# Cross-attention and a ternary feed-forward: the context and Wkv turned by transposes, with work moved between slots and engines

## The chip, the cores and the metric

The kernel runs on one core of one Trainium2 chip. The metric is device microseconds of one execution. The five engines are named as in the profile: PE (TensorE matmul), PEld (TensorE weight load, beside PE), DVE (VectorE), ACT (ScalarE), POOL (GpSimd) and SP (SyncE, which here only starts DMAs).

## What is computed

The input is x, 16 x 56 tokens of 256 channels, and a context whose first 56 rows per batch are used, with 64 channels. The layer is cross-attention and then a feed-forward network whose weights are rounded to -1, 0 and 1 and whose activations are rounded to 8 bits:

```python
kv = latent_kv @ Wkv_expand.T                 # K and V, 256 columns each
k, v = jnp.split(kv, 2, axis=-1)
scores = jnp.einsum('bhqd,bhkd->bhqk', qh, kh) * inv_sqrt_d   # 16 heads of 16, causal
attn = jax.nn.softmax(scores, axis=-1)
x = x + attention(layernorm(x), ctx) @ Wout.T
x = x + qlinear(silu(qlinear(y, w_gate)) * qlinear(y, w_up), w_down)   # y = layernorm(x)
# qlinear: weights round(w / mean|w|) in -1..1, activations round(x * 127 / max|x|)
```

## The kernel before

**Tiles.** The 896 tokens are 7 tiles of 128. Attention goes by 8 pairs of batches (index `u`). The work is cut into slots 0 to 17 and a slot -1 for the start. In slot s below 8 the PE makes `scores(s)`, the transposes of the shifted scores of pair s-1 (`tr`), the products with V (`pv`), the transposes of the attention of pair s-2 (`aT`), the output projection of one token tile (`op`), and the jobs that the table `MISC_JOBS` lists for that slot. From slot 8 on (`GU0`) tile s-8 goes through gate and up products, tile s-10 through the transposes of the rounded gated values (`ht`), and tile s-11 through the down product (`dn`).

**Orders by hand.** Each engine has its own program in a fixed order. The PE writes all small products into four PSUM banks in turn: job number n goes to bank n mod 4 and waits (`take_bank`) until the job four before it has been read. ACT reads a job's bank unless `VECTOR_READS` lists it, in which case DVE does. Both read in the order of the jobs (`read_misc`). A reader of an SBUF tile waits for the bank read that filled it (`wait_read`).

**The start.** Wkv lies in `wkv_sb` with row 4p+o on partition p; the context lies in `ctx_sb` with two key positions of 64 channels side by side. `wkvT` holds Wkv turned, channels on partitions, once on partitions 0 to 63 and once on 64 to 127; `ctxT` holds the context turned, batches 0 to 7 on the lower half of the partitions and 8 to 15 on the upper half. In the kernel before, both are made by matrix products with the identity as moving operand, with an output on either half of the partitions: two jobs `wkvT` (one for K, one for V; 8 products each) and two jobs `ctxT` (4 products each). Each has one read of 128 partitions. An fp32 product stands as two instructions in the trace, a transpose as one.

**Masked K.** The scores need K with other heads set to zero (`k_wide`). For context half 0 the readers of the K products write it from the bank (`WIDE`); for half 1 the product is copied to `kT` and POOL widens it later (`WIDENINGS`).

**Weights.** The three feed-forward weights are loaded by SP (`f0`, `f1`, `f2`), their absolute sums are taken by ACT or DVE (`ABS_SLOTS`), the PE makes the means (`MEAN_SLOTS`), POOL scales and rounds them (`ROUND_SLOTS`), ACT takes the signs (`SIGN_SLOTS`), and three DMA transposes bring them into `wT` and `wdT`. SP's list has one entry `hold`, a wait for Wkv's arrival ahead of the second x load.

**Feed-forward.** Per tile ACT makes silu of the gate product (L677), DVE multiplies by the up product (L885) and takes the maximum (L892), then the tile is rounded in two halves by the engines that `ROUNDER` names (L336), transposed, and multiplied down. `FINISHER` says whether DVE adds scale and residual in one instruction (L925), or ACT scales (L699) and POOL adds (L584).

Of the kernel before, what the change touches and what calls it, by code (L numbers as in the profile page):

```python
# [5 lines left out]
ALU = mybir.AluOpType  # L6
# [53 lines left out]
VECTOR_READS = [('k', 0, (0, 1), (0, 1)), ('xT', 4), ('v', 2), ('q', 1, 2), ('k', 0, (1, 4), (0,)), ('xT', 2), ('xT', 3), ('ctxT', 0),  # L60
 ('k', 1, (0, 4), (0,)), ('woT', 0)]
# [10 lines left out]
SUB_BEHIND = {0: 2, 1: 3, 2: 12, 3: 4}  # L72
# [8 lines left out]
WIDENINGS = {0: [(1, 0, 0)], 1: [], 2: [(1, 1, 0), (1, 1, 1)], 3: [], 4: [(1, 0, 1)], 5: []}  # L81
# [5 lines left out]
ROUNDER = [('gpsimd', 'gpsimd'), ('gpsimd', 'gpsimd'), ('gpsimd', 'gpsimd'), ('gpsimd', 'gpsimd'),  # L87
           ('gpsimd', 'gpsimd'), ('gpsimd', 'gpsimd'), ('vector', 'scalar')]
# [5 lines left out]
FINISHER = ['gpsimd', 'gpsimd', 'gpsimd', 'vector', 'vector', 'vector', 'vector']  # L94
# [6 lines left out]
def xattn_ffn(nc, x, ctx_512, wq, wkv, wout, w_gate, w_up, w_down, out):  # L101
# [72 lines left out]
    with ExitStack() as ctx:  # L174
# [92 lines left out]
        misc_written = sem("misc_written")  # L267

# [72 lines left out]
        def load(eng, name):  # L341
            kind, i = (name[:-1], int(name[-1])) if name[-1].isdigit() else (name, 0)
            if kind == "hold":
                eng.wait_ge(wkv_in, 16)
                return
            if kind == "x":
                a, b = X_PARTS[i]
                eng.dma_start(x_sb[:, a:b, :], x_v[:, a:b, :]).then_inc(x_in[i], 16)
            elif kind == "ctx":
                eng.dma_start(ctx_sb[S // 2 * i:S // 2 * i + S // 2, :, :],  # L350
                              ctx_512[i::4, 0:S, :].rearrange("b (k e) l -> k b (e l)", e=2)).then_inc(ctx_in, 16)
            elif kind == "wkv":
                eng.dma_start(wkv_sb[:, :, :], wkv.rearrange("(p o) c -> p o c", o=4)).then_inc(wkv_in, 16)
            elif kind == "wq":
                eng.dma_start(wq_sb[:, :, :], wq.rearrange("(o p) c -> p o c", p=P)).then_inc(wq_in, 16)
            elif kind == "wo":
# [5 lines left out]

        def read_misc(eng, copy, job):
# [4 lines left out]
            if kind == "wkvT":  # L368
                last = copy(wkvT[:, C * i:C * i + C], bank[:, 0:C])
            elif kind == "ctxT":  # L370
                last = copy(ctxT[:, KT // 2 * i:KT // 2 * i + KT // 2].rearrange("l (k e) -> l e k", e=2),
                            bank[:, 0:KT // 2].rearrange("l (e k) -> l e k", e=2))
# [6 lines left out]
            elif kind == "k" and job in WIDE:  # L379
# [3 lines left out]
                for hf in job[3]:  # L383
                    last = nc.vector.tensor_tensor(k_wide[:, i, hf, :, 2 * S * j0:2 * S * j1],
                                                   bank[:, None, width * (hf - hfs[0]):width * (hf - hfs[0]) + width].to_broadcast([P, RH, width]),
                                                   head_mask[:, 0:RH, None].to_broadcast([P, RH, width]), ALU.mult)
# [579 lines left out]
        def _(pe):  # L966
# [9 lines left out]
            def write_values(i):  # L976
# [3 lines left out]
                wait_read(pe, ("wkvT", 0), ("wkvT", 1), ("ctxT", 0), ("ctxT", 1))  # L980
# [13 lines left out]
            def write_misc(job):  # L994
# [6 lines left out]
                if kind == "wkvT":  # L1001
                    const(pe, "ident")
                    pe.wait_ge(wkv_in, 16)
                    for o in range(4):
                        for c in range(2):
                            last = mm(bank[Q * c:Q * c + Q, o:C:4], wkv_sb[:, o, :], ident[:, Q * i:Q * i + Q],
                                      start=True, stop=True)
                elif kind == "ctxT":
                    pe.wait_ge(ctx_in, 64)
                    for e in range(2):  # L1010
                        for c in range(2):
                            last = mm(bank[Q * c:Q * c + Q, 2 * S * e:2 * S * e + 2 * S],
                                      ctx_sb[:, 2 * c + i, L * e:L * e + L], ident[0:2 * S, 0:2 * S], start=True, stop=True)
                elif kind == "k":
# [3 lines left out]
                    wait_read(pe, ("wkvT", 0), ("ctxT", 0), *[("ctxT", 1)] * (j1 > 2))  # L1018
# [235 lines left out]
```

## Time and profile before

| | us |
|---|---|
| median of 3 runs (88.12 to 88.43) | 88.37 |
| the profiled execution, time | 88.7 |
| its span, first to last instruction | 86.9 |
| PE busy | 79.3 (91%) |
| DVE busy | 69.1 (80%) |
| ACT busy | 53.8 (62%) |
| POOL busy | 48.5 (56%) |

The page gives, for the chain that ended last, PE 57%, DVE 17%, POOL 8%, time without a wait 7%, DMA 4%, ACT 3%. A busy share is a mean over stretches that differ: the page's 40 slices show PE at nine tenths or more nearly to the end, and DVE at nine tenths in the last third. So the rows further down are read by stretch, not from the totals. The profiled execution is 0.33 us above the median; what is worked out from its rows is a difference to it, and is carried over to the median.

### The profile page before, as it was taken

Reading aid. Unit: us, or ns where it says so; the run is one execution under the profiler, and the core shown is the slowest. Engines: PE = TensorE matmul, PEld = TensorE weight load, DVE = VectorE, ACT = ScalarE, POOL = GpSimd, SP = SyncE. Lnnn points to the kernel's source line nnn. Section 1 sums busy time; section 2 is a strip of 40 time slices with the busy share of each in tenths; the row PEclk is TensorE's granted clock in tenths of the full one; section 3 lists DMA queues with packets and bytes.
Section 4 is the critical chain, followed back from the end, with each engine's and each line's share of the span. In section 5 each row is a group of like instructions: output and inputs, shape, how many; then the busy total and the mean of one; then the engine's idle time right before and its main releaser. Section 6 shows DMA issues by size and latency. Waiting matters only on the chain.

```text
span 86.9 us, 2805 instructions
## 1 busy us (share of the span) xinstructions
PE 79.3 (91%) x1068; PEld 57.9 (67%) x1068; DVE 69.1 (80%) x161; ACT 53.8 (62%) x96; POOL 48.5 (56%) x119
## 2 busy tenths in 40 slices
PE   4999999999999999999999899999996989998850
PEld 1387646679888797879888787675642656765630
DVE  4712799699699947999689986659999999999850
ACT  0625321699179737785219997973459969885620
POOL 5640378790891002989469877500989847669000
PEclk9999999999999999999999999999999999999999
DMA  0779999910000000006500092800000000101152
GB/s 26 217 234 316 322 379 370 352 70 8 0 4 8 0 11 0 0 8 130 116 0 8 0 241 55 194 0 0 0 0 0 8 0 0 60 0 60 64 173 69
DMA packets 11748, 7.60 MB, mean 88 GB/s; under 512 B 6552, under 2 KB 11480, under 8 KB 11736
## 3 DMA queue, kind: packets, MB, share of 16 engines
q1 hardware_dynamic: 11068, 6.93, 26.5%
q10 hardware_dynamic: 668, 0.51, 1.9%
q8 instruction: 8, 0.13, 0.6%
q14 instruction: 4, 0.03, 0.1%
HBM read 4.95 MB, written 0.92 MB: 68 GB/s over the span
## 4 chain that ended last, share of the span: by engine, by line
PE 57%; DVE 17%; POOL 8%; issue 7%; DMA 4%; ACT 3%; ACTq 1%; POOLq 0%; DVEq 0%
PE bank L968 32%; PE sc L968 11%; PE bank L1098 6%; DVE amax L892 4%; DVE h_sb L885 4%; DMA ctx_sb<-in_ctx_dram 4%; PE bank L1122 3%; PE bank L1035 2%; ACT hT L623 2%; PE bank L1183 2%; POOL wf_sb L336 2%; POOL wf_sb L572 1%; POOL y_sb L500 1%; DVE shifted L802 1%; POOL rstd L494 1%
## 5 line engine op out<-in xcount | busy, mean ns | idle before, releaser
L968 PE MATMUL sc<-wT,xqT 128*128 128x512 bf16 x56 | 13.7, 380 | 1.5 <-DVE h_sb L885 1.5
L336 POOL TENSOR_SCALAR wf_sb<-h_sb,r_tok 128x512 f32<-128x512 f32 x12 | 8.2, 696 | 7.8 <-DVE r_tok L906 7.5
L677 ACT ACTIVATE wf_sb<-sc,s_out 128x512 f32<-128x512 f32 x14 | 9.6, 692 | 4.0 <-PE sc L968 1.9
L487 POOL TENSOR_SCALAR veps<-mv 128x1 f32<-128x1 f32 x13 | 2.5, 192 | 16.3 <-DVE mv L848 9.3
L885 DVE SCALAR_TENSOR_TENSOR h_sb<-sc,s_out,wf_sb 128x512 f32<-128x512 f32 x14 | 9.9, 745 | 1.1 <-ACT wf_sb L677 1.1
L968 PEld LDWEIGHTS sc<-wT,xqT 128*128 128x128 bf16 x56 | 5.1, 98 | 7.1 <-DVE h_sb L885 2.6
L968 PEld LDWEIGHTS bank<-v_wide,pT 128*64 128x64 f32 x256 | 8.1, 138 | 2.0 <-issue 1.8
L793 DVE TENSOR_REDUCE mx<-sc 128x16 f32<-128x896 f32 x8 | 8.7, 1085 | 0.7 <-PE sc L968 0.7
L968 PE MATMUL bank<-v_wide,pT 128*64 128x34 f32 x256 | 9.0, 225 | 0.0
L413 ACT ACTIVATE pT<-bank 128x448 f32<-128x448 f32 x16 | 7.8, 543 | 1.8 <-PE bank L1098 1.5
L892 DVE TENSOR_REDUCE amax<-h_sb 128x1 f32<-128x1024 f32 x7 | 8.5, 1220 | 0.2
L802 DVE TENSOR_TENSOR shifted<-sc,mx 128x896 f32<-128x896 f32 x8 | 8.7, 1084 | 0.1
L1098 PE MATMUL bank<-ident,shifted 128*128 128x128 f32 x64 | 8.5, 276 | 0.0
L623 ACT ACTIVATE hT<-bank 128x1024 bf16<-128x1024 f16 (+1 forms) x7 | 6.7, 962 | 2.2 <-PE bank L1183 1.7
L968 PE MATMUL bank<-wdT,hT 128*128 128x256 bf16 x56 | 7.3, 272 | 0.9 <-ACT hT L623 0.9
L968 PE MATMUL bank<-xnT,wqT 128*128 128x224 f32 (+1 forms) x40 | 7.5, 330 | 0.1
L968 PE MATMUL bank<-woT,attnT 128*128 128x256 f32 x28 | 7.5, 389 | 0.0
L1098 PEld LDWEIGHTS bank<-ident,shifted 128*128 128x128 f32 x64 | 7.0, 141 | 0.5 <-issue 0.2
L494 POOL TENSOR_TENSOR rstd<-veps,minus_half 128x1 f32<-128x1 f32 x13 | 7.2, 551 | 0.0
L968 PEld LDWEIGHTS bank<-xnT,wqT 128*128 128x128 f32 x40 | 6.2, 190 | 1.1 <-issue 1.0
L572 POOL TENSOR_SCALAR wf_sb<-wf_sb,w_inv 128x1024 f32<-128x1024 f32 x6 | 6.7, 1123 | 0.0
L659 ACT ACTIVATE tern<-wf_sb,minus_magic 128x1024 bf16<-128x1024 f32 x6 | 6.6, 1148 | 0.1
(115 smaller groups left out, 159.2 us busy)
## 6 DMA issues: line engine op xcount, KB each, us to landing
wf_sb<-in_L_ffn_w_gate_dram SPq DMA_DIRECT2D x1, 1024.0 KB, 9.2
wf_sb<-in_L_ffn_w_up_dram SPq DMA_DIRECT2D x1, 1024.0 KB, 11.3
wf_sb<-in_L_ffn_w_down_dram SPq DMA_DIRECT2D x1, 1024.0 KB, 13.0
out_dram<-k_wide SPq DMA_DIRECT2D x7, 128.0 KB, 1.7
x_sb<-in_x_dram SPq DMA_DIRECT2D x1, 512.0 KB, 6.8
wq_sb<-in_L_xattn_Wq_dram ACTq DMA_DIRECT2D x1, 256.0 KB, 3.4
x_sb<-in_x_dram SPq DMA_DIRECT2D x1, 256.0 KB, 4.0
wo_sb<-in_L_xattn_Wout_dram SPq DMA_DIRECT2D x1, 256.0 KB, 9.4
```

The costliest lines, as they stand in the source:

```text
L336: ops.tensor_scalar(h_int[:, t % 2, c, :], h_sb[:, t % 3, GC * c:GC * c + GC], r_tok[:, 1, t:t + 1], CODED, ALU.mult, ALU.add).then_inc(hi ...
L413: last = nc.scalar.activation(pT[:, i % 2, n0:n0 + 4 * 2 * S].rearrange("p (m b q) -> p m b q", m=4, b=2), bank[:, :].rearrange("p (m b q) ...
L494: nc.gpsimd.tensor_tensor(rstd[:, i:i + 1], veps[:, i:i + 1], minus_half[:, 0:1], ALU.pow).then_inc(rstd_ready, 1)
L572: nc.gpsimd.tensor_scalar(piece, piece, w_inv[:, w:w + 1], MAGIC, ALU.mult, ALU.add).then_inc(w_int_ready, 1)
L623: return nc.scalar.activation(dst, src, ACT.Copy, scale=scale, bias=bias)
L677: nc.scalar.activation(g_sb[:, t % 2, GC * c:GC * c + GC], SC[:, j % 4, :], ACT.Silu, scale=s_out[:, 0, t:t + 1]).then_inc(silu_ready, 1)
L793: nc.vector.tensor_reduce(mx[:, u % R, :].rearrange("p (g h) -> p g h", g=NG4), scores_of(), axis=AX_X, op=ALU.max).then_inc(max_ready, 1)
L802: nc.vector.tensor_tensor(shifted[:, u % R, :, 0:S].rearrange("p (g h) k -> p g h k", g=NG4), scores_of(), mx[:, u % R, :].rearrange("p (g ...
L885: nc.vector.scalar_tensor_tensor(h_sb[:, t % 3, cols], SC[:, j % 4, :], s_out[:, 1, t:t + 1], g_sb[:, t % 2, cols], ALU.mult, ALU.mult).th ...
L892: nc.vector.tensor_reduce(amax[:, 1, t:t + 1], h_sb[:, t % 3, :], axis=AX_X, op=ALU.max, apply_absolute_value=True).then_inc(h_amax_ready, 1)
L968: return nc.tensor.matmul(*a, **k)
L1098: last = nc.tensor.transpose(bank[:, P * m:P * m + P], shifted[:, u % R, h0:h0 + 2, :].rearrange("p h k -> p (h k)"), ident[:, :])
```

## The change

- One job `wkvT` of four PE transposes (output 64 partitions x 512) stands for the two jobs of 8 products. ACT reads it in four copies of 64 x 256, each into one half of the partitions (K for the lower half, K for the upper half, V lower, V upper); a new semaphore `wkv_turned` counts the first three, so a K product of half i waits for copy i+1 only.
- Four jobs `ctxT` of one PE transpose each (output 128 x 112) stand for two jobs of four products. Each is read in two copies of 64 x 112, into the half of the partitions that the batch group belongs to. DVE reads the first, ACT the other three.
- The first K product, both column halves, is read into `k_wide` by one DVE instruction in place of two.
- `hold1`: SP starts the gate weights (and all loads behind them) only when the second x load has landed.
- The tables are new: the order of the jobs, who reads which bank, the slots of the absolute sums (up weights: from DVE in slot 2 to ACT in slot 1; down weights: from ACT in slot 3 to DVE in slot 2), means, rounding and signs; in the feed-forward one half of the rounding of tiles 0 to 4 goes from POOL to ACT, the second half of the last tile goes from ACT to POOL, and the finishing of tiles 3 and 5 goes from DVE to ACT and POOL.

```diff
-XQ_SLOTS = [6, 7, 8, 9, 11, 12, 13]
-LN1_SLOTS = {-1: [1, 2, 3, 4, 5], 0: [], 1: [6], 2: [], 3: []}
-ABS_SLOTS = {(0, 'scalar'): [0], (2, 'vector'): [1], (3, 'scalar'): [2]}
-MEAN_SLOTS = [1, 3, 4]
-ROUND_SLOTS = [1, 3, 4, 5, 5, 6]
-SIGN_SLOTS = [4, 4, 6, 6, 6, 7]
+XQ_SLOTS = [6, 6, 8, 9, 10, 12, 13]
+LN1_SLOTS = {-1: [1, 2, 3, 4, 5], 0: [6], 1: [], 2: [], 3: []}
+ABS_SLOTS = {(0, 'scalar'): [0], (1, 'scalar'): [1], (2, 'vector'): [2]}
+MEAN_SLOTS = [1, 4, 4]
+ROUND_SLOTS = [2, 2, 4, 4, 5, 5]
+SIGN_SLOTS = [5, 5, 6, 6, 7, 7]
-SYNC_LOADS = ['x0', 'ctx0', 'ctx1', 'hold', 'x1', 'x2', 'f0', 'wo0', 'f1', 'f2']
+SYNC_LOADS = ['x0', 'ctx0', 'ctx1', 'hold0', 'x1', 'x2', 'hold1', 'f0', 'wo0', 'f1', 'f2']
-MISC_JOBS = {-1: [('wkvT', 0), ('ctxT', 1), ('ctxT', 0), ('xT', 0), ('wqT', 0), ('k', 0, (0, 1), (0, 1)), ('wkvT', 1), ('q', 0, 1),
-      ('k', 1, (0, 4), (1,))],
- 0: [('k', 0, (1, 4), (0,)), ('xT', 1), ('k', 1, (0, 4), (0,)), ('q', 1, 2), ('k', 0, (1, 4), (1,)), ('v', 0), ('v', 2),
+MISC_JOBS = {-1: [('wkvT', 0), ('ctxT', 0), ('ctxT', 1), ('xT', 0), ('wqT', 0), ('ctxT', 2), ('k', 0, (0, 1), (0, 1)), ('q', 0, 1),
+      ('ctxT', 3), ('k', 0, (1, 4), (0,))],
+ 0: [('k', 1, (0, 4), (1,)), ('xT', 1), ('k', 1, (0, 4), (0,)), ('k', 0, (1, 4), (1,)), ('q', 1, 2), ('v', 0), ('v', 2),
      ('xT', 3), ('xT', 2)],
  1: [('q', 2, 4), ('xT', 5)],
- 2: [('v', 1), ('v', 3)],
- 3: [('xT', 4), ('woT', 0), ('xT', 6), ('q', 4, 6)],
+ 2: [('woT', 0), ('v', 1), ('v', 3), ('xT', 4)],
+ 3: [('xT', 6), ('q', 4, 6)],
-VECTOR_READS = [('k', 0, (0, 1), (0, 1)), ('xT', 4), ('v', 2), ('q', 1, 2), ('k', 0, (1, 4), (0,)), ('xT', 2), ('xT', 3), ('ctxT', 0),
- ('k', 1, (0, 4), (0,)), ('woT', 0)]
+VECTOR_READS = [('k', 0, (0, 1), (0, 1)), ('v', 2), ('q', 1, 2), ('xT', 2), ('ctxT', 0), ('xT', 5)]
-SUB_BEHIND = {0: 2, 1: 3, 2: 12, 3: 4}
+SUB_BEHIND = {0: 0, 1: 0, 2: 19, 3: 3}
-WIDENINGS = {0: [(1, 0, 0)], 1: [], 2: [(1, 1, 0), (1, 1, 1)], 3: [], 4: [(1, 0, 1)], 5: []}
+WIDENINGS = {0: [(1, 0, 0), (1, 1, 0)], 1: [], 2: [], 3: [(1, 0, 1)], 4: [(1, 1, 1)], 5: []}
-ROUNDER = [('gpsimd', 'gpsimd'), ('gpsimd', 'gpsimd'), ('gpsimd', 'gpsimd'), ('gpsimd', 'gpsimd'),
-           ('gpsimd', 'gpsimd'), ('gpsimd', 'gpsimd'), ('vector', 'scalar')]
-FINISHER = ['gpsimd', 'gpsimd', 'gpsimd', 'vector', 'vector', 'vector', 'vector']
+ROUNDER = [('gpsimd', 'scalar'), ('scalar', 'gpsimd'), ('gpsimd', 'scalar'), ('gpsimd', 'scalar'), ('gpsimd', 'scalar'),
+ ('gpsimd', 'gpsimd'), ('vector', 'gpsimd')]
+FINISHER = ['gpsimd', 'gpsimd', 'gpsimd', 'gpsimd', 'vector', 'gpsimd', 'vector']
...
             if kind == "hold":
-                eng.wait_ge(wkv_in, 16)
+                eng.wait_ge((wkv_in, x_in[1])[i], 16)
...
             if kind == "wkvT":
-                last = copy(wkvT[:, C * i:C * i + C], bank[:, 0:C])
+                for part in range(4):
+                    values, c = divmod(part, 2)
+                    last = copy(wkvT[Q * c:Q * c + Q, C * values:C * values + C].rearrange("l (p o) -> l o p", o=4),
+                                bank[0:Q, :].rearrange("l (o p) -> l o p", o=4)[:, :, Q * values:Q * values + Q])
+                    if part < 3:
+                        last.then_inc(wkv_turned, 1)
             elif kind == "ctxT":
-                last = copy(ctxT[:, KT // 2 * i:KT // 2 * i + KT // 2].rearrange("l (k e) -> l e k", e=2),
-                            bank[:, 0:KT // 2].rearrange("l (e k) -> l e k", e=2))
+                c, n0 = i // 2, KT // 2 * (i % 2)
+                for e in range(2):
+                    last = copy(ctxT[Q * c:Q * c + Q, n0:n0 + KT // 2].rearrange("l (k e) -> l e k", e=2)[:, e, :],
+                                bank[Q * e:Q * e + Q, 0:2 * S])
...
                     for o in range(4):
-                        for c in range(2):
-                            last = mm(bank[Q * c:Q * c + Q, o:C:4], wkv_sb[:, o, :], ident[:, Q * i:Q * i + Q],
-                                      start=True, stop=True)
+                        last = nc.tensor.transpose(bank[0:Q, P * o:P * o + P], wkv_sb[:, o, :], ident[:, :])
                 elif kind == "ctxT":
                     pe.wait_ge(ctx_in, 64)
-                    for e in range(2):
-                        for c in range(2):
-                            last = mm(bank[Q * c:Q * c + Q, 2 * S * e:2 * S * e + 2 * S],
-                                      ctx_sb[:, 2 * c + i, L * e:L * e + L], ident[0:2 * S, 0:2 * S], start=True, stop=True)
+                    last = nc.tensor.transpose(bank[:, 0:2 * S], ctx_sb[:, i, :], ident[0:2 * S, 0:2 * S])
                 elif kind == "k":
...
-                    wait_read(pe, ("wkvT", 0), ("ctxT", 0), *[("ctxT", 1)] * (j1 > 2))
+                    pe.wait_ge(wkv_turned, i + 1)
+                    wait_read(pe, ("ctxT", 2 * i), *[("ctxT", 2 * i + 1)] * (j1 > 2))
```

## Rows read from the trace of the kernel before

**Rows 1.** Windows: length, PE, PEld, DVE, ACT, POOL busy; clock; DMA share, GB/s

```profile
5.27:11.02 5.75, 5.75 (x53) 4.38 (x53) 2.49 (x10) 2.33 (x6) 1.19 (x4) 1.00 0.94 297
64.30:81.00 16.70, 14.67 (x121) 9.26 (x118) 16.08 (x33) 13.41 (x22) 12.34 (x27) 1.00 0.05 17
```

**Rows 2.** Chain that ended last, in time order: start, length, what

```profile
40.37 2.39 PE bank L968 x12
...
59.03 1.23 DVE amax L892
```

**Rows 3.** Timeline, PE, 1 to 12.7 us: start, length, line, out<-in, form, count

```profile
1.27 2.74 PE L968 MATMUL sc<-tern 128*128 128x512 bf16 x6 [1.27 <-DVE tern L739]
...
3.94 1.12 PE L968 MATMUL bank<-ident,wkv_sb 128*64 128x64 f32 x16
...
5.27 1.75 PE L968 MATMUL bank<-ident,ctx_sb 112*64 112x112 f32 x16 [0.21 <-DMA ctx_sb<-in_ctx_dram]
...
6.95 0.44 PE L1035 MATMUL bank<-ident,xn_sb 128*128 128x128 f32 x2
...
7.23 0.60 PE L1027 MATMUL bank<-ident,wq_sb 128*128 128x128 f32 x4
...
8.38 0.69 PE L968 MATMUL bank<-ident,wkv_sb 128*64 128x64 f32 x16
...
9.00 1.15 PE L968 MATMUL bank<-xnT,wqT 128*128 128x112 f32 x8
...
10.07 1.02 PE L968 MATMUL bank<-ctxT,wkvT 64*128 64x448 f32 x2
...
11.02 0.39 PE L968 MATMUL sc<-causal,sel 64*64 64x224 bf16 x8
...
11.90 0.83 PE L968 MATMUL bank<-ctxT,wkvT 64*128 64x336 f32 x2
...
12.66 0.44 PE L1035 MATMUL bank<-ident,xn_sb 128*128 128x128 f32 x2
```

**Rows 4.** Timeline, ACT

```profile
5.11 0.39 ACT L623 ACTIVATE wkvT<-bank 128x256 f32<-128x256 f32 x1 [0.87 <-PE bank L968]
...
6.33 0.38 ACT L623 ACTIVATE ctxT<-bank 128x224 f32<-128x224 f32 x1 [0.83 <-PE bank L968]
...
7.87 0.60 ACT L623 ACTIVATE wqT<-bank 128x512 f32<-128x512 f32 x1
...
18.14 1.90 ACT L650 ACTIVATE tern<-wf_sb 128x2048 bf16<-128x2048 f32 x1
...
20.02 0.97 ACT L413 ACTIVATE pT<-bank 128x448 f32<-128x448 f32 x2
...
23.80 0.36 ACT L623 ACTIVATE attnT<-bank 128x224 f32<-128x224 f32 x1 [1.83 <-PE bank L1122]
25.70 2.48 ACT L623 ACTIVATE v_wide<-bank,parity_mask 128x512 f32<-128x512 f32 x4 [0.49 <-PE bank L968]
```

**Rows 5.** Timeline, PE, in slot 3

```profile
29.52 0.38 PE L1035 MATMUL bank<-ident,xn_sb 128*128 128x128 f32 x2
30.01 1.75 PE L968 MATMUL bank<-xnT,wqT 128*128 128x224 f32 x8
```

**Rows 6.** Groups by line and form: count, busy, mean ns, idle before

```profile
L623 ACT ACTIVATE w_scale<-bank 128x1 f32<-128x1 f32 x3 | 0.5, 170 | 0.0
...
L623 ACT ACTIVATE wf_sb<-h_sb,r_tok 128x512 f32<-128x512 f32 x1 | 0.7, 724 | 0.1
```

**Rows 7.** Timeline, ACT and DVE in the feed-forward, last tile

```profile
76.26 0.69 ACT L677 ACTIVATE wf_sb<-sc,s_out 128x512 f32<-128x512 f32 x1
...
77.97 1.41 DVE L885 SCALAR_TENSOR_TENSOR h_sb<-sc,s_out,wf_sb 128x512 f32<-128x512 f32 x2
```

**Rows 8.** Timeline, SP: start of the load of the gate weights

```profile
4.64 0.50 SPq L360 DMA_DIRECT2D wf_sb<-in_L_ffn_w_gate_dram  x1
```

**Rows 9.** Page part 6, DMA issues: count, KB each, us to landing

```profile
wf_sb<-in_L_ffn_w_gate_dram SPq DMA_DIRECT2D x1, 1024.0 KB, 9.2
```

More of the change, by code:

```diff
@@ L45 @@
      ('xT', 3), ('xT', 2)],
  1: [('q', 2, 4), ('xT', 5)],
- 2: [('v', 1), ('v', 3)],
- 3: [('xT', 4), ('woT', 0), ('xT', 6), ('q', 4, 6)],
+ 2: [('woT', 0), ('v', 1), ('v', 3), ('xT', 4)],
+ 3: [('xT', 6), ('q', 4, 6)],
  4: [],
- 5: [('q', 6, 8)]}
-VECTOR_READS = [('k', 0, (0, 1), (0, 1)), ('xT', 4), ('v', 2), ('q', 1, 2), ('k', 0, (1, 4), (0,)), ('xT', 2), ('xT', 3), ('ctxT', 0),
- ('k', 1, (0, 4), (0,)), ('woT', 0)]
+ 5: [('q', 6, 8)],
+ 6: []}
+VECTOR_READS = [('k', 0, (0, 1), (0, 1)), ('v', 2), ('q', 1, 2), ('xT', 2), ('ctxT', 0), ('xT', 5)]
@@ L267, in xattn_ffn @@
         misc_written = sem("misc_written")
+        wkv_turned = sem("wkv_turned")
         misc_read = [sem(f"misc_read{i}") for i in range(NB)]
@@ L382, in read_misc @@
                 width = 2 * S * (j1 - j0)
[L383 to L386, printed above, removed]
+                nh = len(hfs)
+                last = nc.vector.tensor_tensor(k_wide[:, i, hfs[0]:hfs[0] + nh, :, 2 * S * j0:2 * S * j1],
+                                               bank[:, 0:nh * width].rearrange("p (i k) -> p i k", i=nh)[:, :, None, :]
+                                               .to_broadcast([P, nh, RH, width]),
+                                               head_mask[:, None, 0:RH, None].to_broadcast([P, nh, RH, width]), ALU.mult)
             elif kind == "k":
@@ L979, in write_values @@
                 assert misc_no[jobs[1]] == misc_no[jobs[0]] + 1
-                wait_read(pe, ("wkvT", 0), ("wkvT", 1), ("ctxT", 0), ("ctxT", 1))
+                wait_read(pe, ("wkvT", 0), *[("ctxT", k) for k in range(4)])
                 pe.wait_ge(pads_ready, 1)
```

## The prediction

> **What bounds the kernel now.** I read the chain of waits first: it runs on the PE from the landing of the context to its last piece there at 40.37 [rows 2], so in the start and the attention slots PE work is worth its full length. The windows confirm it for the start: PE busy 5.75 of 5.75 us while DVE has 2.49 and ACT 2.33 [rows 1]. In the feed-forward the chain changes to DVE (the piece at 59.03) [rows 2], and the window 64.30 to 81.00 shows DVE busy 16.08 of 16.70 us, PE, ACT and POOL each with 2 us or more to spare [rows 1]. So two questions decide: how much earlier the first scores start (11.02 before) [rows 3], and whether anything between there and the feed-forward takes that back. A feed-forward bound by DVE moves as a block.
>
> **The start, step by step.** Times are on the axis of the profiled execution. The PE is at the lower of its two clock levels in the beginning, though the clock column reads 1.00: six products of 512 columns take 2.74 us, about 0.43 apart or 1.2 columns per ns, and the 16 Wkv products take 1.12 us at 3.94 and 0.69 at 8.38 [rows 3]. I assume that the clock rises where it did, between the context products and the second Wkv batch.
>
> Removed on the PE behind the context's landing: the context products, from 5.27 to 6.95, 1.68 us; the second Wkv batch, from 8.38 to 9.00, 0.62; and one K product of 448 columns, from 10.07 to 11.02, 0.95, which goes into slot 0 [rows 3]. Added: four context transposes. Four Wq transposes take 0.60 with their end [rows 3], so 0.11 apart (estimate), twice that at the low level: 0.4 for the first two, 0.2 for the others. Moved in from slot 0: the K product of 336 columns, from 11.90 to 12.66, 0.76 [rows 3]. Sum: -1.68 - 0.62 - 0.95 + 0.6 + 0.76 = -1.9 us.
>
> Against that stand waits for ACT, which now makes ten small copies where it made three. No row shows a copy of 64 partitions that lands on other partitions. By the rows of 128 partitions, 64x256 costs 0.39 [rows 4]; behind one another two ACT copies of 448 take 0.97 and four of 512 take 2.48 [rows 4], so I take 0.31 each for four in a row (estimate). The lower bound for one is 0.17, a copy of one column [rows 6]; the upper bound, if a write to the other half or a step of 16 bytes halved the rate, about 0.7. For 64x112, between 0.17 and the 0.38 of 224 columns [rows 4, 6], I take 0.26. I stay near the rows of the same width, since these copies differ from them only in addresses. Then:
> - Wkv transposes at the low level end about 4.95 (before: 5.06, 3.94 + 1.12 [rows 3]); ACT's four copies run 5.0 to 6.3.
> - Context transposes 5.27 to 5.65, x 5.65 to 6.1, then Wq must wait for its bank, which the fourth Wkv copy frees: 6.4, written 7.2 (0.3 us of waiting).
> - ACT: context copy to 6.7, x to 7.0, Wq 7.25 to 7.85 (0.60 [rows 4], before from 7.87).
> - The q product waits for that read: 7.9 where it was 9.00 [rows 3] (0.25 us of waiting); it takes 1.07 to the next start [rows 3], less where no first weight load is exposed: to 8.8.
> - Last context transpose 0.11, K product 0.76: first scores at 9.7 against 11.02, **1.3 us earlier**. That is -1.9 plus the 0.55 of waits.
>
> DVE's single instruction for the first K product saves under 0.1 us beside this chain: nothing.
>
> **Slots 0 to 7.** Slot 0 of the PE gains the 0.95 product and loses the 0.76 one: 1.1 left. In slot 0 ACT reads what DVE read before, so its absolute sum (1.90 at 18.14 [rows 4]) starts about 0.8 earlier, not 1.1, and the exponentials behind it (20.02 [rows 4]) too; the V products wait for them: 0.8 to 1.0 left. The second absolute sum, 1.90, falls into slot 1 of ACT, where the 1.83 us of idle time ahead of 23.80 [rows 4] cover it to 0.1. If that cover fails, each tenth shows up in the exponentials of slot 2. In slot 2 ACT gets Wout's read (0.60, as Wq's) and one x read ahead of and behind the 2.48 of V reads [rows 4], 1 us more in all, and the transposes of slot 3 need V's bank: some 0.1 of PE waiting. Slot 3 gives back more: the PE started the x transposes at 29.52 and the q product only at 30.01 [rows 5], two transposes taking 0.28 elsewhere (6.95 to 7.23 [rows 3]); that wait of 0.2 goes, since the x tile is read a slot earlier, and one mean (0.14, estimate) moves from slot 3 to slot 4. So about 1.3 stands ahead of the feed-forward. Rounding and signs of the weights move by a slot into idle time of POOL and ACT; the DMA transposes still land ahead of the first gate product.
>
> `hold1` delays the gate weights from 4.64 [rows 8] to the landing of the second x part, an estimated 3 us, but the queue is busy with x until then. They took 9.2 us to land, to 13.8 [rows 8, 9]; their reader comes at about 17.3 after the change. Even all 3 us fit: nothing on the path. The wait also stands ahead of Wout and the other weights on SP, whose readers come later still.
>
> **Feed-forward and end.** A rounding on ACT costs 0.724 [rows 6] per tile for tiles 0 to 4. ACT has 3.3 us to spare in the window [rows 1], but in order: followed through tile by tile, the silu of the last tile starts at 77.2 instead of 76.26 and ends at 77.9, DVE's use of it is at 77.97 [rows 7]. It just fits: nothing, and 0.3 if it slips. POOL's relief buys nothing while DVE is the bound. At the end tile 5 is finished by ACT and POOL behind the last transposes' read, so its store starts some 0.8 us later, right before the last one: 0 to 0.2 us, taken as 0.1.
>
> **Sum:** -1.3 + 0.1 = -1.2 us, 87.5 against the profiled 88.7; carried to the median, 88.37 - 1.2 = 87.2 us. The bounds of the copies (0.17 each: 0.5 more, for the waits vanish; 0.7 each: the four end at 7.8, 1.5 us later, and the gain is gone) give 86.6 to 88.5.
>
> **Rivals.**
> 1. ACT gives it back. For it speaks that the start becomes a chain of ACT copies and that two absolute sums fall in its first two slots; against it the 2.33 us of 5.75 that it was busy [rows 1]. If the PE waits 0.4 us more in slots 1 and 2 and 0.3 in the feed-forward, 87.9.
> 2. The clock rises later: slower. The early PE work that remains ahead of the first K product is transposes with gaps, where there were back-to-back products. If the rise comes only once K and q products have run, at about 10.3, the work from 6.9 to there (about 2.4 us at the high level) takes 4.7; 0.55 of waits and some tails absorb part, the scores start near 10.8, and the time is 88.3. That leaves a gain of 0.2 at the scores, and each us of a still later rise costs half a us there, so from about 10.6 on it decides: at 13 the scores and the next K products run at half speed too, another 1.0 to 1.5 us, 89 to 89.8. For it: the batches at 3.94 and 5.27 ran low, so the rise came only after five us of PE work [rows 3]. Against it: no row shows that a transpose counts less than a product. The Trainium skill, "TensorE: Matmul & The Clock Gate", section "Part 4: PE-mode transpose", says that transposes do not count as PE activity in the way products do; by that rule this change takes early activity away, and this rival would be the result. No stretch of the trace of before tests it.
> 3. The copies between halves are dear, near their upper bound, and the change brings nothing: 88.4.
>
> **How the numbers follow.** Forecast 0.62 (86.4 to 87.7). Rival 1 0.15, at 87.9, half of it beyond the line. Rival 2 0.18, half at 88.3, half at 89 and above. Rival 3 0.05. A measurement here tells 0.5%, 0.44 us, from no change: faster is below 87.93, slower above 88.81. Faster 0.62 + 0.08 = 0.70; same 0.07 + 0.09 + 0.05 = 0.21; slower 0.09. The range 86.3 to 88.4 leaves out the late clock and a larger gain than the bounds give.
>
> **What would show it.** The first scores product on the PE at 9.7 (right), at 10.8 or later with early transposes or q products twice as long (rival 2). ACT's four Wkv copies near 0.31 each and the Wq read at 7.3; copies of 0.6 or more mean rival 3. The q product of slot 3 (30.01 [rows 5]) should still come 1.2 to 1.5 earlier; less means rival 1, and the wait that took it stands in the exponentials of slots 1 and 2. DVE should stay over nine tenths busy in the feed-forward, with its length unchanged. A gain that appears in the feed-forward would prove me wrong about its bound.

## The result, and the profile after

The changed kernel takes **93.56 us** (median of 4, 92.22 to 93.63) where the kernel before takes 88.25 on the same chip: a ratio of **1.054**, interval 1.048 to 1.060. The forecast was 87.2. The profiled execution takes 93.6 us with a span of 91.9. Single executions far above the others of their kernel are left out of all ratios; of all 68 that were timed of the kernel before, 15 lie at 97.6 to 98.4 us.

Lines have moved by the added code: L994 is L968 of before, L649 is L623, L1049 is L1027, L1057 is L1035. The page of after, its PE row and clock row in 40 slices of 2.3 us, tenths:

```profile
PE   4957999999999999999999999899996989998850
...
PEclk9997555557999999999999999999999999999999
```

Before, the clock row is all nines; here slices 5 to 9 are at five, half speed (the lower of the two levels, 1.2 of 2.4 GHz), while the PE row shows nines. The same place in the PE's timeline (start, length, line, out<-in, form, count, idle time before and its releaser), and then one line of before, the second scores:

```profile
3.97 0.97 PE L1031 MATMUL bank<-ident,wkv_sb 128*64 128x128 f32 x4
5.22 0.41 PE L1034 MATMUL bank<-ident,ctx_sb 112*128 112x112 f32 x2 [0.28 <-DMA ctx_sb<-in_ctx_dram]
5.66 0.44 PE L1057 MATMUL bank<-ident,xn_sb 128*128 128x128 f32 x2
7.58 0.66 PE L1049 MATMUL bank<-ident,wq_sb 128*128 128x128 f32 x4 [1.48 <-ACT wkvT L649]
...
8.29 1.20 PE L994 MATMUL bank<-ctxT,wkvT 64*128 64x112 f32 x4
9.42 2.05 PE L994 MATMUL bank<-xnT,wqT 128*128 128x112 f32 x8
...
13.00 0.59 PE L994 MATMUL sc<-causal,sel 64*64 64x224 bf16 x8
...
22.83 0.39 PE L994 MATMUL sc<-causal,sel 64*64 64x224 bf16 x8
```

```profile
17.43 0.39 PE L968 MATMUL sc<-causal,sel 64*64 64x224 bf16 x8
```

and ACT's timeline of after beside it:

```profile
4.98 2.54 ACT L649 ACTIVATE wkvT<-bank 64x256 f32<-64x256 f32 x4 [0.75 <-PE bank L1031]
```

The reader is to see three things. The four Wkv copies take 2.54 us, 0.63 each (before, one copy of 128 partitions took 0.39 [rows 4]). The Wq transposes wait 1.48 us for them. And soon behind that wait the PE runs at half speed: the Wq transposes still take 0.66 (0.60 before), but the first K products take 1.20 and the q products 2.05 (1.15 before, [rows 3]). Ahead of it the clock was up: the x transposes at 5.66 take the 0.44 that they took at the higher level before [rows 3]. So the clock had risen, earlier than in the trace of before, and then **fell**. That it rose earlier isn't the work of the change: e14 below, which starts as the kernel before does, has it up by 5.44, and e6, which starts as the change does, not yet at 5.94. The windows of after (length, busy time of PE, PEld, DVE, ACT, POOL, granted clock, DMA share, GB/s):

```profile
8.00:9.00 1.00, 1.00 (x7) 0.81 (x5) 0.00 (x0) 0.97 (x3) 0.00 (x0) 0.58 0.52 78
...
12.00:20.00 8.00, 8.00 (x56) 3.58 (x56) 3.02 (x6) 3.52 (x9) 6.53 (x18) 0.50 0.89 308
...
21.00:22.00 1.00, 1.00 (x28) 1.00 (x24) 0.17 (x1) 0.00 (x0) 0.60 (x1) 0.59 0.00 0
...
69.30:86.00 16.70, 14.88 (x125) 9.49 (x122) 16.06 (x33) 15.54 (x26) 9.67 (x22) 1.00 0.05 17
```

A mean of 0.58 in the ninth microsecond is 0.16 us at full and the rest at half speed: the fall is at 8.16. By the same sum the rise is at 21.82. In those 13.66 us the PE was busy throughout. All four executions show the low stretch: their mean granted clocks over the whole span are 0.92 to 0.94, where before has 0.99 or more. First scores come at 13.00 (11.02 before, +1.98), second scores at 22.83 (17.43 before, +5.40); the first gate product comes at 60.49 (55.40, +5.09) and DVE's last instruction at 89.21 (84.26, +4.95). All of the loss is made in the first 23 us. The last window answers to [rows 1]: DVE 16.06 of 16.70 us, where it had 16.08.

### The profile page after: what moved, and what is told of

Same layout as the page of the kernel before. It is cut to its first block, busy times and chain, and to the rows that moved or that the text cites. A ratio compares the mean times of both kernels' runs of the same rounds, so it can differ in the third digit from the quotient of the medians.

```text
span 91.9 us, 2735 instructions
## 1 busy us (share of the span) xinstructions
PE 83.0 (90%) x1028; PEld 59.3 (65%) x1028; DVE 66.3 (72%) x155; ACT 60.9 (66%) x114; POOL 47.5 (52%) x117
## 3 DMA queue, kind: packets, MB, share of 16 engines
HBM read 4.95 MB, written 0.92 MB: 64 GB/s over the span
## 4 chain that ended last, share of the span: by engine, by line
PE 77%; DVE 10%; ACT 4%; issue 3%; POOL 2%; POOLq 0%
PE bank L994 39%; PE sc L994 22%; PE bank L1120 6%; ACT wkvT L649 3%; PE bank L1205 3%; PE bank L1144 2%; PE bank L1057 2%; ACT hT L649 2%; DVE h_sb L911 2%; DVE amax L918 1%; PE bank L1049 1%; DVE shifted L828 1%; DVE mx L819 1%; PE bank L1031 1%; DVE amax L880 1%
## 5 line engine op out<-in xcount | busy, mean ns | idle before, releaser
L994 PE MATMUL sc<-wT,xqT 128*128 128x512 bf16 x56 | 13.7, 380 | 1.2 <-DVE h_sb L911 1.2
L354 POOL TENSOR_SCALAR wf_sb<-h_sb,r_tok 128x512 f32<-128x512 f32 x8 | 5.8, 732 | 11.6 <-DVE r_tok L932 11.6
L994 PEld LDWEIGHTS sc<-wT,xqT 128*128 128x128 bf16 x56 | 5.1, 98 | 6.8 <-DVE h_sb L911 2.4
L994 PEld LDWEIGHTS bank<-v_wide,pT 128*64 128x64 f32 x256 | 8.1, 138 | 2.0 <-issue 1.8
L994 PE MATMUL bank<-xnT,wqT 128*128 128x224 f32 (+1 forms) x40 | 9.2, 387 | 0.0
L994 PE MATMUL bank<-v_wide,pT 128*64 128x34 f32 x256 | 9.0, 225 | 0.1
L994 PEld LDWEIGHTS bank<-xnT,wqT 128*128 128x128 f32 x40 | 7.9, 245 | 1.5 <-issue 1.5
L649 ACT ACTIVATE hT<-bank 128x1024 bf16<-128x1024 f16 (+1 forms) x7 | 6.8, 977 | 2.1 <-PE bank L1205 1.9
L994 PE MATMUL bank<-wdT,hT 128*128 128x256 bf16 x56 | 7.2, 272 | 0.9 <-ACT hT L649 0.9
L994 PE MATMUL bank<-woT,attnT 128*128 128x256 f32 x28 | 7.4, 385 | 0.0
## 6 DMA issues: line engine op xcount, KB each, us to landing
wf_sb<-in_L_ffn_w_down_dram SPq DMA_DIRECT2D x1, 1024.0 KB, 10.3
```

The source lines that it names most:

```text
L649: return nc.scalar.activation(dst, src, ACT.Copy, scale=scale, bias=bias)
L994: return nc.tensor.matmul(*a, **k)
```

## The experiments

The theory after the result: the PE's idle time behind ACT's copies makes its clock fall, and the low clock costs more than the wait itself. Rivals: transposes don't hold the clock as products do; or the tables, not the turning, make the loss. Where a kernel here adds PE or ACT instructions, nobody reads their results; none leaves part of the computation out.

**e1: dense copies.** The Wkv transposes write the bank in the order of the channels, so ACT's copies are contiguous on both sides (in the change they read four runs of 64 values and write with a step of 16 bytes).

```diff
-last = nc.tensor.transpose(bank[0:Q, P * o:P * o + P], wkv_sb[:, o, :], ident[:, :])
+last = nc.tensor.transpose(bank[0:Q, o:2 * C:4], wkv_sb[:, o, :], ident[:, :])
...
-last = copy(wkvT[...].rearrange("l (p o) -> l o p", o=4), bank[0:Q, :].rearrange(...)[:, :, Q * values:Q * values + Q])
+last = copy(wkvT[Q * c:Q * c + Q, C * values:C * values + C], bank[0:Q, C * values:C * values + C])
```

> The changed kernel, but the PE writes the turned Wkv with a step of four into the bank, so that ACT's four copies are contiguous on both sides (they took 0.63 us each in the changed kernel, 2.54 in all). Theory 1 (the clock falls because the PE sits idle for 1.5 us behind these copies): copies near 0.31 each, the PE's wait ahead of Wq falls from 1.5 to about 0.3 us, the clock stays at its high level after its rise, first scores at about 9.7, 87.0 to 87.5 us. Theory 2 (it falls because transposes took the place of products, gap or not): the clock still stays or falls low in the start, 91 to 93 us. Theory 3 (the new tables cost, not the start): over 91 us with the clock high.

Measured: 92.51 us, ratio 1.049 (1.045 to 1.054). PE and ACT timelines of e1:

```profile
5.28 0.41 PE L1034 MATMUL bank<-ident,ctx_sb 112*128 112x112 f32 x2 [0.51 <-DMA ctx_sb<-in_ctx_dram]
...
6.44 0.66 PE L1049 MATMUL bank<-ident,wq_sb 128*128 128x128 f32 x4 [0.41 <-ACT wkvT L649]
...
7.96 2.02 PE L994 MATMUL bank<-xnT,wqT 128*128 128x112 f32 x8
```

```profile
4.81 1.58 ACT L649 ACTIVATE wkvT<-bank 64x256 f32<-64x256 f32 x4 [0.58 <-PE bank L1031]
```

The copies fall to 0.39 each, so the reordering cost 0.24 a copy. The copies into the other half of the partitions take as long as those into the same half (0.38 each, without the gaps between them). The wait falls to 0.41. Yet the q products still take 2.02: the clock fell all the same, with 0.92 us of idle time in two pieces. The copies alone are not the loss. The time lies where theory 2 had put it, so this run leaves open whether it is the gaps or the transposes; e3 and e7 decide that.

**e2, e3: the gap filled.** After as it is, with idle products of 512 columns (e2) or fp32 transposes of 128 columns (e3) ahead of the Wq transposes. The two tell idle time from the kind of instruction.

```diff
-WARM_MORE = {}
+WARM_MORE = {('xT', 0): 6}
```

```diff
-WARM_MORE = {}
+WARM_MORE = {('xT', 0): 12}
...
-warm_up(WARM_MORE.get(job, 0))
+for _ in range(WARM_MORE.get(job, 0)):
+    nc.tensor.transpose(SC[:, 3, 0:P], ident[:, :], ident[:, :])
```

> The changed kernel with six more 512-column products into an unused bank behind the transposes of the first x tile, so that the PE works on while ACT copies Wkv. The copies stay dear. Theories 1 and 2: the clock stays high, the first scores come at about 11.2 (13.0 in the changed kernel), 88 to 89 us. Theory 3: over 91 us with a high clock.

> The same gap filled with twelve fp32 transposes of 128 columns in place of the six products (about as long, 1.3 us at the high level). Theory 1, where any PE work counts: as with the products, 88 to 89 us, clock high. Theory 2, where transposes don't count: the clock falls as in the changed kernel, 92 to 94 us.

Measured: **87.47 us** with products, ratio 0.992 (0.990 to 0.995), and **87.67 us** with transposes, 0.993 (0.991 to 0.996). PE timelines of e2, then of e3:

```profile
6.09 1.46 PE L994 MATMUL sc<-tern 128*128 128x512 bf16 x6
7.52 0.66 PE L1049 MATMUL bank<-ident,wq_sb 128*128 128x128 f32 x4
...
10.94 0.39 PE L994 MATMUL sc<-causal,sel 64*64 64x224 bf16 x8
```

```profile
6.15 1.47 PE L1174 MATMUL sc<-ident 128*128 128x128 f32 x12
7.54 0.66 PE L1049 MATMUL bank<-ident,wq_sb 128*128 128x128 f32 x4
```

The Wq transposes start when they did (7.52 and 7.54, 7.58 in after), so the copies are as dear as ever and Wq starts no earlier. Only the gap is gone, and 6 us with it: the times are below the 88 to 89 us expected. Products and transposes do the same: none of the ten executions of the two has a mean granted clock under 0.99.

**e4: the tables alone.** Wkv and the context turned by products as before and no `hold1`, all other tables of after.

```diff
-MISC_JOBS = {-1: [('wkvT', 0), ('ctxT', 0), ('ctxT', 1), ('xT', 0), ('wqT', 0), ('ctxT', 2), ('k', 0, (0, 1), (0, 1)), ('q', 0, 1),
-      ('ctxT', 3), ('k', 0, (1, 4), (0,))],
+MISC_JOBS = {-1: [('wkvT', 0), ('ctxT', 1), ('ctxT', 0), ('xT', 0), ('wqT', 0), ('k', 0, (0, 1), (0, 1)), ('wkvT', 1), ('q', 0, 1),
+      ('k', 0, (1, 4), (0,))],
```

> The kernel before (Wkv and context turned by products, two jobs each, early hold only) with all the other tables of the change: order of the jobs, readers, slots of the weights' steps, widenings, rounders, finishers. Theories 1 and 2: the clock as before, the start 0.2 us shorter by the swapped K products, 0.3 to 0.5 us gained in slots 1 to 3, nothing in the feed-forward: 87.5 to 88.0 us. Theory 3: the tables alone cost several us, over 91.

Measured: 87.54 us, ratio 0.994 (0.991 to 0.996). The tables make no loss; first scores at 10.75, second at 16.59. That slot 0 is shorter than before (5.84 against 6.41) the prediction had not said; e13 and e14 take it up.

**e5: a gap in the kernel before.** Ten idle copies on ACT ahead of the first Wkv read, no new transposes.

```diff
+for r in range(10 if i == 0 else 0):
+    copy(h_sb[:, r // 4, C * (r % 4):C * (r % 4) + C], bank[:, 0:C])
 last = copy(wkvT[:, C * i:C * i + C], bank[:, 0:C])
```

> The kernel before, with ten more ACT copies of the first Wkv bank (into a tile that is not in use yet) ahead of the one that counts, so that the PE, which turns everything by products as ever, must wait some 1.5 us ahead of the Wq transposes. Idle theory (the clock falls when the PE stands idle in the stretch behind its rise, whatever it worked on): the clock falls, 92 to 95 us. Transpose theory (it falls because products were replaced by transposes): the clock stays, only the wait itself is paid, 89 to 90 us.

Measured: 98.73, 90.19, 98.61 and 98.94 us, too far apart for a ratio. PE timeline of the profiled one, and a window of it:

```profile
8.31 1.12 PE L1029 MATMUL bank<-ident,wq_sb 128*128 128x128 f32 x4 [0.37 <-ACT wkvT L625]
...
11.53 2.05 PE L970 MATMUL bank<-xnT,wqT 128*128 128x112 f32 x8
...
27.47 0.64 PE L970 MATMUL sc<-k_wide,qT 32*64 32x112 f32 x32
```

```profile
8.31:27.39 19.08, 19.08 (x134) 11.79 (x134) 8.53 (x20) 5.07 (x12) 8.17 (x21) 1.00 0.52 179
```

With no transpose added, the PE stays at half speed until 27.4: Wq takes 1.12, q 2.05. The window's clock reads 1.00 all the same: a stretch ahead of the first rise shows no lower value in this column, and only the lengths tell. But this run doesn't decide between the theories. The clock had not risen when the added wait came, so it could not fall behind it, and at half speed that wait was only 0.37 us (0.50 stood ahead of the context products). Nor does it show that the added wait kept the clock down: three of four executions lie near 98.7 us, and the kernel before, without the wait, has 15 of 68 near 98, of which no trace is kept. The fourth, 90.19 us at a mean clock of 1.00, is 2 us above before, which is about what the wait alone was to cost. What the trace does show is what a late rise costs: some 10 us, the wait included.

**e6, e7: dense copies and the gaps filled.** e1 with a few idle products (e6) or transposes (e7) behind three jobs; the transposes are written by e3's loop.

```diff
-WARM_MORE = {}
+WARM_MORE = {('wkvT', 0): 1, ('xT', 0): 2, ('k', 0, (0, 1), (0, 1)): 1}
```

```diff
-WARM_MORE = {}
+WARM_MORE = {('wkvT', 0): 2, ('xT', 0): 4, ('k', 0, (0, 1), (0, 1)): 2}
```

> The contiguous copies of e1, plus four 512-column products in the PE's waits: one behind the Wkv transposes, two behind the first x transposes, one behind the first K product. Both theories: the clock stays high, first scores at 9.7 (10.9 in e2), 86.2 to 86.8 us. A fall of the clock would mean that neither the idle time nor the kind of work decides.

> The same with fp32 transposes of 128 columns in the waits, two for each product (about as long). Idle theory: as e6, 86.2 to 87.0 us, clock high. Transpose theory: hardly a product is left in the stretch from 4.5 to 7.2 us, the clock falls as in e1, 92 to 94 us.

Measured: 86.59 us, 0.983 (0.980 to 0.985), and **86.67 us**, 0.983 (0.980 to 0.985). PE timelines of e6 (two lines), then of e7:

```profile
5.94 0.63 PE L1057 MATMUL bank<-ident,xn_sb 128*128 128x128 f32 x2
...
10.41 0.39 PE L994 MATMUL sc<-causal,sel 64*64 64x224 bf16 x8
```

```profile
4.64 0.38 PE L1174 MATMUL sc<-ident 128*128 128x128 f32 x2
5.27 0.41 PE L1034 MATMUL bank<-ident,ctx_sb 112*128 112x112 f32 x2 [0.25 <-DMA ctx_sb<-in_ctx_dram]
5.53 0.44 PE L1057 MATMUL bank<-ident,xn_sb 128*128 128x128 f32 x2
5.81 0.60 PE L1174 MATMUL sc<-ident 128*128 128x128 f32 x4
6.48 0.66 PE L1049 MATMUL bank<-ident,wq_sb 128*128 128x128 f32 x4
...
7.16 0.69 PE L994 MATMUL bank<-ctxT,wkvT 64*128 64x112 f32 x4
...
9.90 0.39 PE L994 MATMUL sc<-causal,sel 64*64 64x224 bf16 x8
...
12.10 1.02 PE L994 MATMUL bank<-ctxT,wkvT 64*128 64x448 f32 x4
```

From 4.64 to 7.16 the PE of e7 does nothing but transposes, and the clock is at the higher level (x in 0.44, Wq in 0.66) and stays there. No execution of e6 or e7 has a mean granted clock under 0.99. The Trainium skill's sentence that transposes don't count as PE activity in the way products do ("TensorE: Matmul & The Clock Gate", section "Part 4: PE-mode transpose") is not borne out here; e3 says the same. e6 missed one expectation: its first scores come at 10.41, not 9.7; in its trace the clock was not up yet at the x transposes (0.63).

**e8, e12, e15: the new turning in the tables of before.** e8 is e7 with before's tables (and without `hold1`). In e12 two K products change places, as the change has them. In e15 ACT reads the moved one in place of DVE.

```diff
-      ('ctxT', 3), ('k', 1, (0, 4), (1,))],
- 0: [('k', 0, (1, 4), (0,)), ('xT', 1), ...
+      ('ctxT', 3), ('k', 0, (1, 4), (0,))],
+ 0: [('k', 1, (0, 4), (1,)), ('xT', 1), ...
```

```diff
-VECTOR_READS = [..., ('q', 1, 2), ('k', 0, (1, 4), (0,)), ('xT', 2), ...
+VECTOR_READS = [..., ('q', 1, 2), ('xT', 2), ...
```

> e7's way of turning (transposes, contiguous copies, transposes in the waits) in the tables of the kernel before: the other half to e4. If the two parts add up (e4 gained 0.6, e7 1.55 us), this gains 0.9: 87.2 to 87.5 us, first scores at about 10.1, clock high. Over 88: the turning is worth nothing by itself, and the gain of e7 lies in the tables' use of it.

> The kernel of e8 (new turning in the tables of before), with two K products in each other's place, as the change has them: the product for context half 0 (336 columns) is the last job of the start, that for half 1 (448 columns) the first of slot 0. Theory: what made e8 slower than before is the wait of 1.11 us behind the last context transpose (the K product for half 1 needs its copy, the one for half 0 does not). Then that wait falls to 0.2 us or less, the first scores start near 10.4 instead of 11.69 (1.11 of waiting and 0.2 of product length less), and the time is 87.5 to 88.1 us. Rival: the loss is in the tables of the slots behind the start (who reads and takes which sum); then the scores come earlier but slots 0 to 2 give it back and the time stays at 88.7 to 89.2.

> The kernel of e12 with one read moved: ACT, not DVE, reads the K product of 336 columns at the end of the start. Theory: in e12 that read of 0.86 us stood ahead of DVE's statistics of x, x came 1.8 us later than in e8, and the PE waited 1.66 us for it, behind which its clock fell. Then the statistics start near 8.5, the wait is under 0.3, the clock stays at the higher level, and with the first scores at 9.8 the time is 86.9 to 87.6. Rival: the clock falls anyway, since the start has too little PE work ahead of slot 0: 91 or more.

Measured: e8 89.02 us, 1.006 (1.004 to 1.009); e12 **92.28 us**, 1.044 (1.033 to 1.054); e15 87.8 us, 0.995 (0.991 to 0.999). PE timeline of e8, then PE, POOL and DVE of e12, then two windows of e12:

```profile
5.82 0.64 PE L1057 MATMUL bank<-ident,xn_sb 128*128 128x128 f32 x2
...
6.99 0.60 PE L1049 MATMUL bank<-ident,wq_sb 128*128 128x128 f32 x4
...
10.78 0.99 PE L994 MATMUL bank<-ctxT,wkvT 64*128 64x448 f32 x2 [1.11 <-ACT ctxT L649]
```

```profile
5.50 0.41 PE L1034 MATMUL bank<-ident,ctx_sb 112*128 112x112 f32 x2 [0.78 <-DMA ctx_sb<-in_ctx_dram]
...
9.76 0.39 PE L994 MATMUL sc<-causal,sel 64*64 64x224 bf16 x8
...
13.32 0.41 PE L1057 MATMUL bank<-ident,xn_sb 128*128 128x128 f32 x2 [1.66 <-POOL xn_sb L526]
...
14.95 2.05 PE L994 MATMUL bank<-xnT,wqT 128*128 128x112 f32 x8
```

```profile
12.63 0.55 POOL L526 TENSOR_SCALAR xn_sb<-x_sb,negm,rstd 128x256 f32<-128x256 f32 x1 [0.19 <-POOL rstd L520]
```

```profile
9.87 0.86 DVE L409 TENSOR_TENSOR k_wide<-bank,head_mask 128x672 f32<-128x672 f32 x1 [1.48 <-PE bank L994]
...
10.79 0.37 DVE L780 BATCH_NORM_STATS2 stats<-x_sb 128x6 f32<-128x256 f32 x1
```

```profile
14.00:14.50 0.50, 0.50 (x2) 0.00 (x0) 0.45 (x1) 0.15 (x1) 0.31 (x2) 0.70 1.11 352
...
21.00:21.50 0.50, 0.50 (x10) 0.14 (x8) 0.50 (x2) 0.50 (x2) 0.24 (x1) 0.97 0.00 0
```

e8 missed the 87.2 to 87.5 expected. In its start the PE makes transposes alone from 3.89 to 7.62, and the clock even rises among them (x in 0.64, Wq in 0.60). The K product of half 1 stands right behind the last context transpose and waits 1.11 us for its copy. The profiled execution keeps its clock behind that wait; three of the ten, at 93.4 to 94.9 us, have a mean granted clock of 0.93 to 0.94, as the executions of after have. e12 was to take that wait away, and did: first scores at 9.76 in place of 11.69. The expected time was still missed by over 4 us, since DVE now reads the moved product ahead of its statistics of x; these start at 10.79 (9.03 in e8), POOL's normalized x comes at 13.18, the PE waits 1.66 us, and its clock falls at 14.2 and is back at 21.03. This is the fall of after once more, with another releaser; all four executions of e12 have a mean clock of 0.94 to 0.96. e15 takes the read from DVE: statistics at 8.78, no PE wait over 0.22 from the Wq transposes to the second scores, clock high, 87.8 (a little over what I expected). Swap and reader belong together.

**e13, e14: the pair.** e13 is e7 with the q product put back between two K products of slot 0; e14 is the kernel before with only these two put side by side.

```diff
- 0: [..., ('k', 1, (0, 4), (0,)), ('k', 0, (1, 4), (1,)), ('q', 1, 2), ...
+ 0: [..., ('k', 1, (0, 4), (0,)), ('q', 1, 2), ('k', 0, (1, 4), (1,)), ...
```

> The kernel of e7 with one change in the order of slot 0: the q product stands between the K product of half 1 (448 columns) and that of half 0 (336 columns), as it did before. Theory: next to each other these two run at the same time, since they use different halves of the partitions; parted, the shorter one costs its own 0.76 us again. Then slot 0 (first scores to second scores on the PE) grows from 5.85 to 6.6 us, and the time from 86.67 to 87.2 to 87.5. Rival: the shorter slot 0 of the new order comes from who reads the banks, not from the pair; then slot 0 stays at 5.8 to 6.0 and the time within 0.2 of 86.67.

> The kernel before with one change: in slot 0 the K product of half 0 (336 columns) goes ahead of the q product, right behind that of half 1 (448 columns). Theory (the pair runs at the same time): slot 0 falls from 6.41 to about 5.7 us, and the time by 0.5 to 0.8, to 87.4 to 87.8, nearly all that the tables alone gave in e4 (87.54). Rival: no change in slot 0, 88.1 to 88.4.

Measured: e13 87.19 us, 0.986 (0.980 to 0.993); e14 88.93 us (87.86 to 90.18), 0.999 (0.994 to 1.005). PE timeline of e13, then of e14:

```profile
12.35 1.02 PE L994 MATMUL bank<-ctxT,wkvT 64*128 64x448 f32 x2
13.29 1.15 PE L994 MATMUL bank<-xnT,wqT 128*128 128x112 f32 x8
14.37 0.83 PE L994 MATMUL bank<-ctxT,wkvT 64*128 64x336 f32 x2
...
16.75 0.39 PE L994 MATMUL sc<-causal,sel 64*64 64x224 bf16 x8
```

```profile
5.44 0.99 PE L968 MATMUL bank<-ident,ctx_sb 112*64 112x112 f32 x16 [0.37 <-DMA ctx_sb<-in_ctx_dram]
...
10.42 0.39 PE L968 MATMUL sc<-causal,sel 64*64 64x224 bf16 x8
...
12.44 1.02 PE L968 MATMUL bank<-ctxT,wkvT 64*128 64x448 f32 x4
13.64 1.15 PE L968 MATMUL bank<-xnT,wqT 128*128 128x112 f32 x8 [0.19 <-DVE k_wide L384]
```

Parted, 448 and 336 columns take 1.02 and 0.83; side by side, all four instructions take 1.02 (the line x4 of e7 and of e14). Slot 0 is 6.60 in e13 and 5.85 in e7. It is the rows that show the pair: the ratios of e13 and e7 have intervals that overlap. In e14 slot 0 is 5.92, with 0.19 of a new wait, against 6.41 before; but the 0.5 to 0.8 us expected of the time is not shown, its executions lie too far apart. e14 shows something else: with the start of the kernel before its clock is up at 5.44, for the context products take 0.99 where before had 1.75 [rows 3], and its first scores come at 10.42 in place of 11.02.

**e9, e10, e11: what is off the path, and a better version.** e7 with before's `ROUNDER` and `FINISHER` (e9); without `hold1` (e10); with Wkv read in two copies of 64 x 512 in place of four, and one idle transpose in place of four behind the first x (e11; only the copies are shown below).

```diff
...
-FINISHER = ['gpsimd', 'gpsimd', 'gpsimd', 'gpsimd', 'vector', 'gpsimd', 'vector']
+FINISHER = ['gpsimd', 'gpsimd', 'gpsimd', 'vector', 'vector', 'vector', 'vector']
```

```diff
-SYNC_LOADS = ['x0', 'ctx0', 'ctx1', 'hold0', 'x1', 'x2', 'hold1', 'f0', 'wo0', 'f1', 'f2']
+SYNC_LOADS = ['x0', 'ctx0', 'ctx1', 'hold0', 'x1', 'x2', 'f0', 'wo0', 'f1', 'f2']
```

```diff
-for part in range(4):
-    values, c = divmod(part, 2)
-    last = copy(wkvT[Q * c:Q * c + Q, C * values:C * values + C], bank[0:Q, C * values:C * values + C])
+for c in range(2):
+    last = copy(wkvT[Q * c:Q * c + Q, :], bank[0:Q, :])
```

> e7 with the rounding and finishing of the feed-forward as in the kernel before. My theory (the feed-forward is bound by DVE, the move of work from POOL to ACT is worth nothing, the later finish of tile 5 costs 0 to 0.2): within 0.3 of e7, 86.3 to 86.9 us. Rival (part of e7's gain lies there): 87.0 or more.

> e7 without the second hold, so that SP starts the weights right behind the x loads. My theory (the hold is off the path): within 0.2 of e7, 86.4 to 86.9 us. Rival (the held weights let x land earlier and that is part of the gain): x lands 1 us or more later, DVE's first moments wait for it, 87.0 or more.

> e7 with Wkv read in two copies of 64x512 (0.59 each by the Wq read) in place of four of 64x256 (1.58 in all in e1): 0.4 us less on ACT ahead of the Wq transposes, and one transpose in the PE's wait behind the first x in place of four. If the ACT chain still sets the start, the first scores come 0.2 to 0.4 us earlier than e7's 9.9, 86.2 to 86.5 us; if the PE sets it, the same as e7.

Measured: e9 86.77 us, 0.983 (0.979 to 0.986); e10 86.61, 0.981 (0.978 to 0.985): both as e7. e11 **86.24 us**, 0.978 (0.974 to 0.981), faster than both kernels: ACT reads Wkv in 1.21 us, and the first scores come at 9.57.

## Why the prediction was wrong, step by step

**The copies** were a mis-sized term: 0.31 each in the sum, 0.63 measured. The upper bound (0.7, "a step of 16 bytes") had the cause, and e1 shows it: 0.39 when both sides are contiguous, and even that is over 0.31. Rival 3's sign, copies of 0.6 or more, came, but not its price of 88.4: with the clock held and the copies dear, e2 takes 87.47; dense copies bring 0.9 us more (e6). So the reordering was worth 0.9 us, not 6.

**The clock** is the step that failed. "I assume that the clock rises where it did" looked at the rise only. The clock fell again, behind waits that I had let in at the price of their own length. Better copies would not have saved the forecast: e1's wait ahead of Wq (0.41) is near the 0.3 that I had priced, its other wait (0.51) is for the context's landing, and e1 still loses 4.3 us. Rival 2 had the right engine and the wrong mechanism: it made the rise late because early products became transposes, and e3 and e7 show that transposes hold the clock. Its signs came (first scores behind 10.8, q products twice as long), and its price, 89 to 89.8, was short by 4 us: it let the low level end at about 13 at the latest, and it lasted to 21.82 with the PE busy. Its own sum did not come out either: 4.7 us of work from 6.9 ends at 11.6, not at 10.3. At half speed slot 0 took 9.83 us where e7 takes 5.85.

**The start** came near only in other kernels and by luck: 9.7 was forecast, e7 has 9.90 and e11 9.57, but there the copies are dense, the waits are filled, and the clock was up by 5.3. With a rise as late as I had assumed, e6 has 10.41; with dear copies, e2 has 10.94; after itself 13.00. Like with like, the new start brings some 0.6 us with a late rise (e6 against before, 11.02) and 0.5 with an early one (e7 against e14, 10.42), not 1.3. These are single executions.

**Slot 0** was wrong: I had it 0.2 longer (0.95 in, 0.76 out), and it is 0.56 shorter in e7. I took the K products one by one; the new order puts two of different partition halves side by side, and the 336 columns cost nothing (0.75 us of slot 0, e13 against e7). The Trainium skill ("TensorE: Matmul & The Clock Gate", section "Part 3: Packing small matmuls — row/col tiling") says that products on different row groups run at the same time, and the trace agrees: 1.02 us for the four instructions.

**Slots 1 to 3** came as forecast in kind, with other sizes: the second absolute sum is covered (slot 1 is 0.05 longer in e7), slot 2 is 0.78 longer, slot 3 is 1.36 shorter. Slots 4 and 6, of which I had said nothing, are 0.26 and 0.33 longer; why is not shown. The q product of slot 3 starts at 28.07 in e7, 1.94 earlier than before [rows 5], where 1.2 to 1.5 was expected, so rival 1 (ACT gives it back) is out.

**Feed-forward and weights**: right. DVE's window keeps its share, e9 and e10 bring no change.

**The sum** was -1.2 us; with the clock held it is about -1.5 (0.0173 of 88.3, e7). That this is near is partly luck: the start gave less than I had it, and the pair that I had missed is in it. The parts don't add: tables alone 0.6 us (e4), turning alone 0.5 lost (e8), or 0.4 gained with two entries of the tables set right (e15), both 1.5.

**Left open**: how much idle time is too much. Pieces of 0.51 and 0.41 us were enough in e1, while 0.78 us in e12, ahead of its context transposes, did no harm, and 1.11 us in one piece left the clock high in seven of e8's ten executions and, by their mean clock, not in the other three. Nor is it shown why the first rise comes before 5.5 us in some executions (e7, e14), near 6.9 in others with the same start (e6, before) and at 27.4 in e5, or why the low stretch lasted 13.66 us in after and 6.83 in e12.

## What to carry to other kernels

Price a new wait on the PE twice: by its length, and by what all PE work behind it costs at half speed; if it falls into the start or the slots right behind it, fill it with idle products or transposes, whichever are at hand. Before a start is compared in two traces, see whether the clock had risen at the same place in both. When an order by hand changes, look at which products become neighbours on different partition halves, and who reads a moved product, not only at the count of instructions. Let the PE write a bank in the order that the reader wants, since the copy that reorders is the one that is waited for.

## What the runs showed of the hardware that I had not expected

- A clock that has risen can fall behind waits of about half a microsecond (0.51 and 0.41, e1), though a wait of 1.11 us did not always make it fall (e8); it stayed low for 13.66 us (after) or 6.83 us (e12) with the PE busy all the while.
- fp32 transposes kept the clock high as products did (e2 against e3, e6 against e7), and it rose among transposes alone (e8).
- With the same start the first rise differs by some 1.5 us from one execution to another: the context products take 1.75 at 5.27 in before and 0.99 at 5.44 in e14.
- The clock column shows 1.00 ahead of the first rise, even for 19 us at half speed (e5).
- An fp32 ACT copy of 64 x 256 that reorders, writing with a step of 16 bytes, takes 0.63 us, a contiguous one 0.39 (e1); landing on the other half of the partitions adds nothing that shows.
- Two K products on different partition halves that stand side by side take the time of the longer one, 1.02 us against 1.02 and 0.83 (e7, e13).
